# Macaron kernel on Trainium2: the first routing moved between the shared units, its bias on a semaphore of its own, weight splits moved into the first pair

## What is computed

```
x = x + 0.5 * ffn(layernorm(x))
x = x + attention(layernorm(x))      # no softmax: 32 heads of size 4, (q k^T) v, then a group norm
x = x + 0.5 * ffn(layernorm(x))

ffn(x):                              # x is (tokens, 128)
  scores = sigmoid(x @ router_w.T)   # 16 experts in 4 groups of 4
  s = scores + bias                  # used for choosing only
  keep the 2 groups with the largest sum of their two best s, then the 4 best experts
  tw = 2.5 * scores[chosen] / (sum of them + 1e-20)
  routed = sum over experts e of combine[:, e] * ((silu(x @ gate_w[e]) * (x @ up_w[e])) @ down_w[e])
  shared = (silu(x @ sh_gate_w) * (x @ sh_up_w)) @ sh_down_w     # 256 wide
  return routed + shared
```

## Time and profile before

| | |
|---|---|
| median of 3 runs | 751.8 us (751.61 to 751.99) |
| the profiled execution, its own time | 755.5 us |
| its span in the profile | 753.8 us |
| PE busy | 90% of the span |
| DVE busy | 79% |
| POOL busy | 57% |
| ACT busy | 53% |
| mean granted TensorE clock | 0.965 of full |
| DMA | 76.4 MB, mean 101 GB/s |

### The profile page before, as it was taken

One profiled execution on the slowest core, in us unless ns is written; L12 is line 12 of the kernel. 1 busy time (PEld: TensorE's weight loads), 2 busy tenths in 40 slices (PEclk: granted clock), 3 DMA queues, 4 the chain that ended last, 5 costly groups with the idle time before them and its releaser, 6 DMA issues.

```text
span 753.8 us, 12004 instructions
## 1 busy us (share of the span) xinstructions
PE 680.1 (90%) x3116; PEld 555.4 (74%) x3116; DVE 592.5 (79%) x1571; ACT 397.6 (53%) x784; POOL 432.1 (57%) x373
## 2 busy tenths in 40 slices
PE   3498989989898988989979989799897999989897
PEld 2287778878787877778867878678686878878675
DVE  3898696878887697886878878878788797878674
ACT  3464645555573543755436554366553655555453
POOL 4555655666673553855547455475553766666564
PEclk9799999999998998999989999899998999999999
DMA  6640606041230601405006051050410606041240
GB/s 189 191 168 2 224 1 225 1 180 46 98 129 0 225 2 31 195 0 224 0 5 221 0 194 45 3 223 14 174 65 0 225 15 225 15 168 72 66 174 15
DMA packets 30789, 76.37 MB, mean 101 GB/s; under 512 B 3968, under 2 KB 12688, under 8 KB 30736
## 3 DMA queue, kind: packets, MB, share of 16 engines
q1 hardware_dynamic: 30736, 75.81, 28.0%
HBM read 73.18 MB, written 2.62 MB: 101 GB/s over the span
## 4 chain that ended last, share of the span: by engine, by line
PE 33%; DVE 21%; issue 20%; POOL 18%; DMA 4%; ACT 2%; POOLq 1%; SPq 0%; DVEq 0%; ACTq 0%
POOL A_lo L323 16%; DVE T L952 6%; DVE A L974 5%; PE gateP L410 4%; PE gateP L412 3%; PE gateP L411 3%; PE yP L410 3%; PE yP L411 3%; PE yP L412 3%; PE upP L412 3%; PE upP L411 3%; PE upP L410 3%; DMA CB<-combT 2%; DVE wsum L841 2%; DMA ebias<-in_L_ffn_bias_dram 1%
## 5 line engine op out<-in xcount | busy, mean ns | idle before, releaser
L323 POOL TENSOR_TENSOR A_lo<-A,A_hi 128x512 fp32r<-128x512 f32 x288 | 371.5, 1295 | 252.7 <-ACT A_hi L673 252.6
L656 ACT ACTIVATE gateP<-gateP 128x512 f32<-128x512 f32 x256 | 149.0, 582 | 232.1 <-PE gateP L412 231.6
L952 DVE TENSOR_TENSOR T<-gateP,CB 128x512 f32<-128x512 f32 x256 | 175.3, 685 | 103.9 <-ACT gateP L656 81.1
L673 ACT CAST A_hi<-A 128x512 fp32r<-128x512 f32 x288 | 176.6, 613 | 42.6 <-DVE A L974 42.6
L974 DVE TENSOR_TENSOR A<-upP,T 128x512 f32<-128x512 f32 x256 | 177.0, 691 | 9.1
L410 PE MATMUL gateP<-XT_hi,W_hi 128*128 128x512 f32 x288 | 124.6, 433 | 3.5 <-DVE T L952 3.1
L410 PE MATMUL yP<-A_hi,W_hi 128*128 128x512 f32 x288 | 115.0, 399 | 1.5 <-ACT YT L589 0.9
L410 PE MATMUL upP<-XT_hi,W_hi 128*128 128x512 f32 x288 | 115.5, 401 | 0.3
L412 PE MATMUL gateP<-XT_lo,W_hi 128*128 128x512 f32 x288 | 115.4, 401 | 0.0
L411 PE MATMUL gateP<-XT_hi,W_lo 128*128 128x512 f32 x288 | 115.3, 400 | 0.0
L412 PE MATMUL upP<-XT_lo,W_hi 128*128 128x512 f32 x288 | 114.6, 398 | 0.0
(11 more groups left out here) (169 smaller groups left out, 671.6 us busy)
## 6 DMA issues: line engine op xcount, KB each, us to landing
CB<-combT SPq DMA_DIRECT2D x128, 512.0 KB, 7.1
out_dram<-X SPq DMA_DIRECT2D x8, 256.0 KB, 2.0
X<-in_L_attn_x_dram SPq DMA_DIRECT2D x3, 512.0 KB, 6.1
W_in<-in_L_ffn_gate_w_dram SPq DMA_DIRECT2D x4, 256.0 KB, 5.3
W_in<-in_L_ffn_up_w_dram SPq DMA_DIRECT2D x4, 256.0 KB, 5.3
W_in<-in_L_ffn_down_w_dram SPq DMA_DIRECT2D x4, 256.0 KB, 5.4
X<-in_L_attn_x_dram SPq DMA_DIRECT2D x2, 256.0 KB, 3.7
combT<-CT SPq DMA_DIRECT2D x16, 32.0 KB, 1.8
```

Source lines behind the costliest of these rows:

```text
L323: pool.tensor_tensor(A_lo[:, slot, :], A[:, slot, :], A_hi[:, slot, :].bitcast(F32), ALU.subtract).then_inc(low_done, 1)
L656: act.activation(dst, gateP[u % 2][:, :], ACT.Silu).then_inc(silu_done, 1)
L673: act.copy(A_hi[:, v % SLOTS, :], A[:, v % SLOTS, :]).then_inc(high_done, 1)
L952: dve.tensor_tensor(T[:, u % TS, :], gateP[u % 2][:, :], CB[:, e, :], ALU.mult).then_inc(gate_weighted, 1)
```

## The change

- ebias gets its own semaphore `ebias_in`, and its load is issued behind the three shared weight loads instead of ahead of them. PE waits for the router weights alone; DVE waits for ebias ahead of routing part 0.
- ACT runs the first `normalise` ahead of the copy of RT.
- DVE runs parts 0 and 1 of the first routing ahead of the first pair, parts 2 to 4 behind the multiply of unit 0, parts 5 to 7 behind the multiply of unit 1.
- PE's `transpose_weights(0)` and ACT's `copy_weights(0)` stand at u = 3 instead of u = 1.
- ACT makes W_hi of units 0 to 3 ahead of the pair (before: 0 to 9), of 4 to 9 at u = 0 to 2, two each, and of 10 to 17 at u = 3 to 10 (before: u = 0 to 7). POOL still makes W_lo of units 0 to 9 ahead of its first pair. DVE makes W_lo of 10 to 17 at u = 3 to 10 (before: u = 0 to 7).
- blkm is made at u = 35 of the first pair instead of ahead of the first routing.

```diff
--- before.py
+++ after.py
@@ -210,6 +210,7 @@
         x_first, x_rest = sem("x_first"), sem("x_rest")
         w_in = [sem(f"w_in{i}") for i in range(1 + E // ESEM)]
         router_in, small_in = sem("router_in"), sem("small_in")
+        ebias_in = sem("ebias_in")
         const_seq = sem("const_seq")
         w_hi_done, w_lo_done, w_lo_late = sem("w_hi_done"), sem("w_lo_done"), sem("w_lo_late")
         setup_psum, setup_sb = sem("setup_psum"), sem("setup_sb")
@@ -246,14 +247,14 @@
         def _(sp):
             sp.dma_start(X[:, 0:TILES, :], x_v[0][:, 0:TILES, :]).then_inc(x_first, 16)
             sp.dma_start(R_in[:, :], router_w).then_inc(router_in, 16)
-            sp.dma_start(ebias[:, :, :], bias.unsqueeze(0).unsqueeze(0).broadcast_to([P, TILES, E])
-                         ).then_inc(router_in, 16)
 
             for i, w in enumerate((sh_gate_w, sh_up_w)):
                 sp.dma_start(W_in[:, 0:SHARED, i, :],
                              w.rearrange("d (s f) -> d s f", s=SHARED)).then_inc(w_in[0], 16)
             sp.dma_start(W_in[:, 0:SHARED, 2, :],
                          sh_down_w.rearrange("(s f) d -> f s d", s=SHARED)).then_inc(w_in[0], 16)
+            sp.dma_start(ebias[:, :, :], bias.unsqueeze(0).unsqueeze(0).broadcast_to([P, TILES, E])
+                         ).then_inc(ebias_in, 16)
             for g in range(E // ESEM):
                 for i, w in enumerate((gate_w, up_w, down_w)):
                     sp.dma_start(W_in[:, SHARED + g * ESEM:SHARED + (g + 1) * ESEM, i, :],
@@ -538,7 +539,7 @@
 
                             pe.wait_ge(attended, 2 * (p - ATT0 + 1))
                         transpose_back(t0 + s - 1)
-                    if first and u == 1:
+                    if first and u == 3:
                         transpose_weights(0)
                     if first and u == 6:
 
@@ -558,7 +559,7 @@
 
 
             pe.wait_ge(const_seq, IDENT_AT)
-            pe.wait_ge(router_in, 32)
+            pe.wait_ge(router_in, 16)
             pe.transpose(attP[:, 3 * P:3 * P + E], R_in[:, :], ident[0:E, 0:E]).then_inc(setup_psum, 1)
             transpose_next(0)
             pe.wait_ge(setup_sb, 1)
@@ -654,7 +655,10 @@
                         else:
                             dst = gateP[u % 2][:, :]
                         act.activation(dst, gateP[u % 2][:, :], ACT.Silu).then_inc(silu_done, 1)
-                    if first and u == 1:
+                    if first and u < 3:
+                        for unit in range(4 + 2 * u, 6 + 2 * u):
+                            split_high(unit)
+                    if first and u == 3:
                         copy_weights(0)
                     if first and u == 7:
 
@@ -662,8 +666,8 @@
                         act.wait_ge(setup_psum, 2)
                         for i, matrix in enumerate((WkT, WvT, WoT)):
                             act.copy(matrix[:, :], attP[:, i * P:(i + 1) * P]).then_inc(setup_sb, 1)
-                    if first and u + AHEAD < UNITS:
-                        split_high(u + AHEAD)
+                    if first and 3 <= u < 3 + UNITS - AHEAD:
+                        split_high(u - 3 + AHEAD)
                     if u <= PAIR and not (first and u == 0):
                         v = u - 1
                         act.wait_ge(mul_done, n + v + 1)
@@ -687,15 +691,15 @@
             act.wait_ge(const_seq, 2)
             act.activation(warm[:, :], half[:, 0:1], ACT.Silu)
 
+            normalise(0, 0, 0)
+            normalise(0, 0, 1)
             act.wait_ge(setup_psum, 1)
             act.copy(RT[:, :], attP[:, 3 * P:3 * P + E]).then_inc(setup_sb, 1)
-            normalise(0, 0, 0)
-            normalise(0, 0, 1)
             next_high(0, 0)
             for unit in range(SHARED):
                 split_high(unit)
             route_silu(0)
-            for unit in range(SHARED, AHEAD):
+            for unit in range(SHARED, 2 * SHARED):
                 split_high(unit)
             pair(0, True, False, False)
             for p in range(1, ATT0):
@@ -973,6 +977,15 @@
                         dve.wait_ge(low_done, n + u + 1 - SLOTS)
                     dve.tensor_tensor(A[:, u % SLOTS, :], upP[u % 2][:, :], gated,
                                       ALU.mult).then_inc(mul_done, 1)
+                    if first and u < 2:
+                        for part in range(2, 5) if u == 0 else range(5, 8):
+                            if part in (5, 6):
+
+                                dve.wait_ge(route_seq, 21 if part == 5 else 22)
+                            route(0, part)
+                    if first and u == PAIR - 1:
+                        dve.tensor_scalar(blkm[:, :], blk1[:, :], 1.0 / HEAD, None,
+                                          ALU.mult).then_inc(attended, 2)
                     if w == 7 and not (first and s == 0):
                         residual(t0 + s - 1, 2 * ((p - 1 + s) % BATCH) + (1 - s))
                     if not (last and s == 1):
@@ -988,8 +1001,8 @@
                             next_full(t)
                         if 8 <= w < 16:
                             route(t, w - 8)
-                    if first and u + AHEAD < UNITS:
-                        split_low(u + AHEAD)
+                    if first and 3 <= u < 3 + UNITS - AHEAD:
+                        split_low(u - 3 + AHEAD)
                     if attention:
                         attention_stage(u, p - ATT0)
 
@@ -997,18 +1010,14 @@
             dve.wait_ge(x_first, 16)
             stats(0, 0)
             next_full(0)
-            dve.wait_ge(router_in, 32)
             dve.wait_ge(const_seq, CONSTS)
 
             dve.wait_ge(xt_hi_ready, 1)
             dve.tensor_tensor(XT_lo[:, 0, :], XT[:, :], XT_hi[:, 0, :].bitcast(F32),
                               ALU.subtract).then_inc(xt_lo_ready, 1)
 
-            dve.tensor_scalar(blkm[:, :], blk1[:, :], 1.0 / HEAD, None, ALU.mult).then_inc(attended, 2)
-            for part in range(8):
-                if part in (5, 6):
-
-                    dve.wait_ge(route_seq, 21 if part == 5 else 22)
+            dve.wait_ge(ebias_in, 16)
+            for part in range(2):
                 route(0, part)
             pair(0, True, False, False)
             for p in range(1, ATT0):
```

## The result

The changed kernel takes 756.65 us (median of 6 runs, 754.83 to 757.41) against 751.89 us for the kernel before (6 runs beside it, lowest 751.04): ratio 1.006, 95% interval 1.0044 to 1.0077, slower by 4.8 us. Forecast was 756.6. The profiled execution took 756.26 us, its span is 754.5.

What follows compares the result with a forecast made beforehand. No engine is full; PE's wait for comb, the routing's result, sets the time. A later comb (+3.0) and late weight splits (+1.8) add 4.8 us to the median 751.8, giving 756.6; range 753.0 to 759.6.

Steps and rivals of the forecast that it cites:

- The head start of 3.7 us: First step: normalise at 6.7 instead of 10.4, first routing instruction at 12.6, the gain absorbed by waiting for X.
- Parts 0 to 4 done before X: DVE, first routing: these parts and the multiply of unit 0 end at 24.4, before X lands at 26.6.
- The wait for X: DVE ahead of step 1's stats: waits for the last X load until 26.6, with parts 5 to 7 queued behind.
- Stats 1.75, multiply 0.68, parts 5 to 7 3.27: DVE after X lands at 26.6: these durations bring comb to 32.3 if nothing holds them.
- Holds of 1.4 us: DVE, first routing: hot held 0.95 and wsel some 0.5 us by POOL's first two A_lo, comb at 33.7.
- The first term: First step: comb at 33.7 instead of 30.68, +3.0 us, with bounds -0.3 and +4.1.
- Late splits +1.8: DVE, u = 8 to 10: three W_lo splits at the median 608 ns delay comb of step 1; bounds +1.1 and +4.1.
- Sum: Whole kernel: +3.0 and +1.8 make +4.8 us, median 756.6, with steps 1 to 15 unchanged.
- the faster case: Rival, first step: X is there when DVE asks, comb at best 24.1, -4.8 us, 747.0; chance 0.05.
- The splits did not collide: Rival, units 8 to 16: each of three W_lo splits held by an A_lo, +7.1 us in all, 758.9; chance 0.12.
- The rival by which nothing arrives: Later steps: wsum, said held in 15 of 16 routings, gives back 0.97 each; five cancel the sum, 751.8; chance 0.07.

Runs made afterwards that it cites:

- the early splits: Changed kernel, with DVE's W_lo of units 10 to 17 at u = 1 to 7 instead of 3 to 10; ratio 1.0044 to the kernel before.
- The experiment with an own semaphore: Changed kernel, with the second block of batch 0 of X on its own semaphore; median 754.9 us, ratio 1.0003 to the kernel before.
- A_lo was moved: Changed kernel, with POOL making the first two A_lo only when comb of step 0 is done; ratio 1.0078 to the kernel before.
- the kernel with the bias edits alone: Kernel before, with only the bias semaphore, later ebias load and normalise ahead of the RT copy; 748.1 against 752.7 us, ratio 0.9963.

## Why the prediction was right

- **The head start of 3.7 us**: measured 3.5 (16.23 to 12.71 by the timeline), and absorbed as forecast. The bias landed at 12.7 (forecast 11.9), late enough to hold near for 1.04 us, which the wait for X covered.
- **Parts 0 to 4 done before X**: bound 24.4, measured 24.97. The bound was slightly low, since DVE had to wait 1.81 us for the Silu of unit 0 ahead of its multiply; the conclusion stands.
- **The wait for X**: forecast end 26.6, measured 27.65. I had argued that the bytes ahead are the same. They are, but they move later. In every kernel here there is a slow stretch about the bias load: before from 3 to 8 us, in the changed kernel from 5 to 12. By 12 us the DMA engines had moved 126 GB/s x 12 = 1.51 MB before and 96 x 12 = 1.15 MB after (rows below); the missing 0.36 MB at the 309 GB/s that follow are some 1.2 us, an estimate, against the 1.1 that were missed. This is argued and not shown: with the early splits 112 GB/s x 12 = 1.34 MB were moved by 12 us, which by the same estimate would be 0.5 us, and the wait ended at 27.71 too. The term was undersized by 1.1 us. Nor does the later issue of the last X load (20.7 instead of 19.0) set it: with the early splits the three loads begin to be issued at 18.75 instead of 19.40. The experiment with an own semaphore shows the wait as cause: 2.4 of the 3.7 us at T of unit 2. The first 12 us, of before and of after:

```profile
0.00:12.00 12.00, 0.26 (x1) 0.18 (x1) 1.83 (x12) 3.20 (x7) 5.38 (x18) 1.00 0.46 126
```

```profile
0.00:12.00 12.00, 3.01 (x13) 2.56 (x13) 3.21 (x14) 4.63 (x10) 6.01 (x19) 1.00 0.39 96
```

- **Stats 1.75, multiply 0.68, parts 5 to 7 3.27**: vareps ends at 29.44, 1.76 behind 27.68; the rest as worked out.
- **Holds of 1.4 us**: hot +0.78, wsel +0.49, together 1.27, and gone when A_lo was moved. Here the row of 16 free executions spoke for none and the held sel row for some. The sel row was the right neighbour. In the trace of before no A_lo ran when hot started, in any of the 16: in 11 it started 0.11 to 0.36 us behind hot, in 5 none ran beside it. In the changed kernel the first pair of A_lo started 0.36 us ahead of hot. The Trainium skill, SBUF — State Buffer, section Who interferes with whom, says that a DVE instruction with two SBUF inputs contends with a GpSimd instruction that reads SBUF, and that issue order decides who blocks; the trace agrees (hot 1.20 us behind A_lo, 0.42 ahead of it).
- **The first term** came to +3.7 at T of unit 2 (forecast +3.0), by the late X.
- **Late splits +1.8**: by the marks +2.0 behind T of unit 2 (35.0 against 33.0), but only 1.4 of it is the splits'. That much lies in units 8 to 16, where three splits of 0.50 to 0.55 us were added to an engine without a gap, and it is 1.4 in every experiment. The median of 608 ns was the wrong row for them: it takes in splits of 0.66 to 1.36 us, and none of the three was held. The other 0.6 lies in units 2 to 7, where there is one split fewer than before; it is the granted clock behind the wait for CB, which the sum had at nothing.
- **Sum**: +4.8 forecast. Measured +3.7 and +1.4 and +0.6 are the +5.7 at comb of step 1; +5.0 is left at steps 3 to 5, +4.8 in the medians. The mechanism of the two terms was right, the first 0.7 too small and the second 0.4 too large, and a third was missing. That the last figure is met to 0.1 us is luck: the interval on it is 3.3 to 5.8 us.
- **Rivals**: the wait for X bound, so the faster case never opened. Its price of -4.8 was wrong as well: with an own semaphore X is there when DVE asks (25.20, no wait), and T of unit 2 is still 1.3 us and comb of step 1 3.7 us later than before. That case rested on parts 0 to 4 ending as early as 18.4 without holds, and they kept most of them. What the earlier start is worth when the routing and the splits stay where they were, the kernel with the bias edits alone shows: 0.9963. The splits did not collide. The rival by which nothing arrives read its row wrongly: wsum is held in 11 of the 16 routings of before and free in 5, not held in 15 (the row gives a minimum and a median, no count), and in the changed kernel it is again held in 11. Of the 0.7 us given back between steps 1 and 3, none is the clock, since both traces have one dip of the same size there (a step of 42.66 us before and 42.65 after, at 0.96). It lies in step 1 to 2 of the kernel before, which takes 41.69 us at full clock where 41.03 is usual; why is open.

What stays open: what sets how long the clock stays at its lower level behind the wait for CB (7 to 14 slow matmuls, in one trace per kernel), and whether the early splits or the freed hot reach the end, which the scatter of times hides.

## What to carry to other kernels

When work is cut into parts and laid between other work, read what the list already holds between them: here a wait for four loads, harmless behind the routing, came in front of its last three parts. A semaphore that counts several loads makes the first user wait for the last of them, so give the piece that is needed first its own. And an edit that makes a result earlier is worth what the next list allows: ACT's copy, SP's issue list and the attention loads each took the gain in turn until they were moved too. A mark behind a long wait of TensorE also carries the clock: count its slow matmuls before a difference is put down to the edit.

## What the runs showed of the hardware that I had not expected

- About the load of the bias (512 pieces of 64 bytes, 32 KB) the DMA engines move little and SP stands at the loads behind it, wherever it is put: before, SP stood 2.12 and 2.73 us at the last two loads of the first expert group; with the bias behind the shared weights, 3.90 us at the X load that follows them. At 9.9 us the changed kernel's list is still 0.5 us ahead; it falls behind at the next two issues (1.34 and 1.78 us instead of 0.43 and 0.51). That the small pieces are the cause is inferred from the stretch moving with the load; no run changed their size.
- Small DVE instructions of 128x16 to 128x64 were held at most one per POOL instruction: 0.16 to 0.23 us became 0.92 to 1.04 beside W_lo (two took 0.54 and 0.61), also a scalar_tensor_tensor with two inputs from SBUF (masked, 0.92 us in the bias-only kernel). Reading PSUM beside the same W_lo was free: the multiply of unit 0 took 0.69 us.
- How long the granted clock stays at half behind a wait differs: between 7 and 14 matmuls behind the wait for CB were slow, though its products there are the same, and units 2 to 7 took 13.7 to 15.3 us by it (22.3 where another wait fell among them).
- The step with a granted-clock dip (0.69 over 9.6 us) took 2.7 us more in the one execution than in the other, more than half of the effect under study.
